# Attention and two mixture layers on one core: row numbers copied by VectorE, block 1 mixed ahead of the first bend

## What is computed

```python
# layer 0, after the attention; x: (16, 128, 128)
topk_val, topk_idx = lax.top_k(x @ gate_w + gate_b, 2)
combine = sum(one_hot(topk_idx, 24) * softmax(topk_val)[..., None], axis=-2)
h = gelu(einsum('bsd,edf->besf', x, w1) + b1)          # 24 experts, 128 -> 512
y = einsum('besf,efd->besd', h, w2) + b2               # 512 -> 128
x2 = x_in + einsum('bse,besd->bsd', combine, y) + x
# layer 1
scores = einsum('bsa,a->bs', tanh(x2 @ W1 + b1), v)
p = softmax(where(mask, scores[:, None, :], -1e30), axis=-1)
pooled = einsum('bjl,bld->bjd', p, x2) / cnt
# then 8 experts of width 176 (two for each token) and a shared network on pooled, added to x2
```

## Time and profile before

| what | us |
|---|---|
| median of 3 runs | 454.02 |
| lowest and highest run | 451.75, 457.33 |
| span of the profiled execution | 429.2 |
| busy: PE, DVE, ACT, POOL | 375.2, 278.9, 247.4, 197.5 |

### The profile page before, as it was taken

How to read it: one execution, slowest core, us unless ns; L and a number is a source line. 1 busy time by engine, 2 the same in 40 slices (tenths; PEclk the granted TensorE clock), 3 DMA queues, 4 the chain that set the end, 5 groups by cost and what they waited for, 6 DMA issues and landing times.

```text
span 429.2 us, 10202 instructions
## 1 busy us (share of the span) xinstructions
PE 375.2 (87%) x2637; PEld 270.4 (63%) x2637; DVE 278.9 (65%) x1132; ACT 247.4 (58%) x743; POOL 197.5 (46%) x273
## 2 busy tenths in 40 slices
PE   4999999899999995799998998479988779899960
PEld 4456556556666652689998997145565457677650
DVE  4566888888878888376555666369566536365562
ACT  2688788788887891546555564328874124344420
POOL 5421254444334434544554555223737506466561
PEclk9999999999999996599999999569999999899995
DMA  7603999678888404467767675320101122232354
GB/s 150 95 15 97 391 279 251 165 166 199 195 204 182 89 20 136 113 160 180 215 165 199 173 175 155 106 94 21 57 26 52 48 52 72 69 79 76 81 172 147
DMA packets 61072, 57.14 MB, mean 133 GB/s; under 512 B 6042, under 2 KB 49703, under 8 KB 60768
## 3 DMA queue, kind: packets, MB, share of 16 engines
q1 hardware_dynamic: 56288, 48.10, 45.1%
q0 software_dynamic: 4736, 8.47, 5.8%
HBM read 36.12 MB, written 21.73 MB: 135 GB/s over the span
## 4 chain that ended last, share of the span: by engine, by line
PE 58%; issue 12%; DMA 9%; DVE 8%; POOL 6%; ACT 4%; SPq 1%; POOLq 1%; DVEq 0%; ACTq 0%
PE bank L764 13%; PE bank L773 6%; PE bank L896 5%; PE bank L787 5%; PE bank L901 5%; DMA layer_outputs<-w_all 3%; POOL layer_outputs L744 3%; PE bank L1023 3%; DMA w_all<-layer_rows 2%; POOL layer_outputs L702 2%; PE bank L1103 2%; DMA qexp<-layer_outputs 2%; PE bank L804 2%; PE bank L818 2%; PE bank L871 2%
## 5 line engine op out<-in xcount | busy, mean ns | idle before, releaser
L1151 ACT ACTIVATE ps<-bank,ntop 128x128 f32<-128x128 f32 x256 | 73.4, 378 | 11.8 <-DVE ntop L1414 10.1
L1218 ACT ACTIVATE hT<-bank,w 128x128 f32<-128x128 f32 x176 | 50.8, 368 | 40.4 <-PE bank L896 40.1
L764 PE MATMUL bank<-qexp 128*128 128x512 f32 x128 | 67.8, 612 | 0.5 <-ACT ps L1151 0.5
L744 POOL DMA_INDIRECT layer_outputs<-w_all x40 | 39.9, 997 | 39.1 <-DVE w_all L1917 21.7
L773 PEld LDWEIGHTS bank<-ident,ps 128*128 128x128 f32 x256 | 31.9, 141 | 33.3 <-issue 29.8
L896 PE MATMUL bank<-xT,w 128*128 128x128 f32 x352 | 49.1, 284 | 2.8 <-DMA w<-in_L_ffn_w_dram 1.2
L1160 ACT ACTIVATE pT<-bank 128x512 f32<-128x512 f32 x64 | 38.6, 603 | 19.1 <-PE bank L773 18.1
L1413 DVE TENSOR_REDUCE mx<-bank 128x4 f32<-128x512 f32 x64 | 43.7, 683 | 8.5 <-PE bank L764 7.0
L668 POOL TENSOR_TENSOR qexp<-kA,rowmask 128x512 f32<-128x512 f32 x15 | 15.6, 1037 | 69.1 <-DVE kA L1498 69.1
L896 PEld LDWEIGHTS bank<-xT,w 128*128 128x128 f32 x352 | 44.6, 199 | 4.0 <-issue 2.6
L732 POOL DMA_INDIRECT layer_rows<-rows_all,places x32 | 30.8, 961 | 24.7 <-DVE rows_all L1791 10.3
(11 more groups left out here) (328 smaller groups left out, 814.6 us busy)
## 6 DMA issues: line engine op xcount, KB each, us to landing
w<-in_L_ffn_w_dram SPq DMA_DIRECT2D x44, 258.0 KB, 3.4
layer_rows<-fill SPq DMA_DIRECT2D x10, 910.0 KB, 9.1
w_all<-in_L_ffn_w_dram SPq DMA_DIRECT2D x24, 256.0 KB, 4.7
qexp<-layer_outputs SPq DMA_DIRECT2D x8, 512.0 KB, 4.0
xt<-layer_rows SPq DMA_DIRECT2D x45, 65.0 KB
w_all<-layer_rows SPq DMA_DIRECT2D x40, 65.0 KB, 1.9
xfT<-in_xfT_dram SPq DMA_DIRECT2D x16, 128.0 KB, 2.4
layer_rows<-fill SPq DMA_DIRECT2D x1, 1560.0 KB, 12.3
```

What stands on the lines that cost most here:

```text
L744: g.indirect_dma_start(ys1_dram, bass.IndirectOffsetOnAxis(ap=xt1[r][:, P:P + 1].bitcast(U32), axis=0), yb1[r][:, :], None, bounds_check=Y ...
L764: pe.matmul(psA[g % 2][:, :], qexp[b % 2][:, g, :], kexp[b % 2].rearrange("p g k -> p (g k)"), start=True, stop=True).then_inc(a_in_ps, 1)
L1151: m = s.activation(ps[g % 2][:, t, :], psA[g % 2][:, t * P:(t + 1) * P], ACT.Exp, bias=ntop[:, h:h + 1])
L1218: s.activation(hT[r % 2][:, c, :], banks[c][:, 0:P], ACT.Gelu, bias=w1[r][:, F0 + c:F0 + c + 1]).then_inc(gelu_done, 1)
```

## The change

It has two parts. In the extra tiles the copy of the row numbers moves from GpSimd, where it followed the send of the tile before, to VectorE, where it stands ahead of the result of the same tile; the semaphore `copied` goes. In the middle stage VectorE mixes block 1 ahead of `bend(0)` and not behind the two memsets that follow it, and `mixing` gets a wait for its own results of the block before (`x2_ready`).

```diff
             nr = pool.value_load(rounds[0:1, 0:1], min_val=EXTRA_MIN // RING, max_val=EXTRA_MAX // RING)
-            g.tensor_copy(row_r[0][:, :], idx[:, E0:E0 + 1]).then_inc(copied, 1)
             with pool.Fori(0, nr) as n:
                 for r in ring:
-                    j = RING * n + r
-                    pool.wait_ge(y_ready, E0 + 1 + j)
-                    pool.wait_ge(copied, j + 1)
+                    pool.wait_ge(y_ready, E0 + 1 + RING * n + r)
                     carry(pool)
                     send_results(row_r[r][:, 0:1], r)
-                    q = (r + 1) % RING
-                    pool.wait_ge(y_out[q], 16 * (E0 // RING + n + (r + 1) // RING))
-                    g.tensor_copy(row_r[q][:, :], idx[:, bass.ds(j + E0 + 1, 1)]).then_inc(copied, 1)
...
             def extra_y(n, r):
-                dve.wait_ge(weights_kept, 2 * (RING * n + r + 2))
+                j = RING * n + r
+                dve.wait_ge(weights_kept, 2 * (j + 2))
+                dve.wait_ge(y_out[r], 16 * (n + first_extra))
+                dve.wait_ge(xT_ready, E0 + j + 1)
+                carry(dve)
+                v.tensor_copy(row_r[r][:, :], idx[:, E0 + j:E0 + j + 1] if isinstance(j, int) else idx[:, bass.ds(E0 + j, 1)])
                 take_y(E0 + RING * n + r, r, n + first_extra, b2_r[r])
...
                 dve.wait_ge(xa_ready, k + 1)
+                if k >= 1:
+                    dve.wait_ge(x2_ready, k)
                 for t in range(BLK):
...
             mixing(0)
+            mixing(1)
             cb.join()
             bend(0)
             for t in ht1:
                 v.memset(t[:, F1:2 * P], 0.0).then_inc(ht1_zero, 1)
             dve.wait_ge(ht1_zero, 2)
-            mixing(1)
             weigh(0)
```

More of the change, by code:

```diff
@@ L317, in attention_moe_kernel @@
         lists_full = sem("lists_full")
-        copied = sem("copied")
         xt_in = [sem(f"xt_in{r}") for r in range(RING)]
```

## The result

| | before | after |
|---|---|---|
| median of 20 runs each, us | 454.50 | 459.07 |
| lowest and highest | 449.88, 457.99 | 453.57, 466.02 |
| span of the profiled execution | 429.2 | 459.5 |

The ratio is 1.0092 with a 95% interval of 1.0061 to 1.0123: 4.6 us slower by the medians, where 0.7 was forecast with a range up to 457.8. It lies within 2%, but outside the range. Runs of one kernel fall into a faster and a slower group, and every ratio in this document is that of the fast ones alone, so it isn't the quotient of the medians beside it.

What follows compares the result with a forecast made beforehand. It took the seam into the second layer to be bound by GpSimd's last send, block 1's load and mixing(1), not PE. Terms -3.65, +3.25 and +1.10 gave +0.7 us, 454.7 us from 454.0, range 451.4 to 457.8.

Steps and rivals of the forecast that it cites:

- The send 3.65 us earlier: End of the extra tiles: without its copy GpSimd starts the last send at 268.1 in place of 271.75.
- I cost the extra tiles at nothing: Extra tiles: VectorE's added copies, taken as 0.2 us each, are hidden in its spare time and add nothing.
- the last send near 268.1: Sign at the loop's end: GpSimd's last send starts there, or 1.0 to 1.6 us after the last result starts.
- the last result at 266.6: Sign at the loop's end: VectorE's last extra result still starts at this time, within 0.2 us.
- rival 4: Extra tiles: VectorE becomes the bound if its copy costs up to 1.04 us; 11 us more, 465 us, chance 0.03.
- rival 3: Extra tiles: sends held by copies of the second weights, so GpSimd still lags; +4.3 us, 458.3 us, chance 0.12.
- 3.25 + 1.10: Seam, us added at PE: bend and exponentials behind block 1's mixing, then GpSimd's addition in VectorE's way.
- `mixing(1)` at 274.4: Seam: block 1's load and mixing move along with the last send, so mixing starts 3.65 us before 278.08.
- The round of bend and exponentials behind M: Seam: bend(0) through exponentials, 3.10 us, now follows M, the end of block 1's mixing (277.55); costs 3.25 us.
- The collision: Seam: GpSimd's residual addition for block 3 holds up weigh(0)'s first VectorE operation; PE starts 1.10 us later.
- The clock: PE behind the seam: full clock may return later relative to the work, adding 0 to 0.5 us; outside the sum.
- The descriptor rule: Extra tiles: by the skill page, VectorE's SBUF copies block GpSimd's descriptor writes, some 2.5 us more per send; not adopted.

Runs made afterwards that it cites:

- e_dummy: Kernel before plus a VectorE copy of the row numbers ahead of each extra tile's result, into a spare tile nobody reads; ratio 0.9937, repeat 1.0005.
- c_before: Kernel before, unchanged, run and profiled a second time; median 451.39 us against 452.65 for the kernel before beside it, ratio 1.0003.
- c_after: Changed kernel with both parts, run and profiled a second time; median 460.69 us against 452.65 for the kernel before, ratio 1.0140.
- e_afill: Changed kernel plus two unread matmuls on PE between turn_x2(1) and turn_weights(0); median 454.90 us against 452.63 for the kernel before, ratio 1.0092.

## Why the prediction failed

- **The send 3.65 us earlier: wrong, by the term "I cost the extra tiles at nothing".** The steps on GpSimd held: a send starts 1.15 us after its result (1.06 forecast), none waits for a copy, and it follows the send before after 0.30 (0.64 assumed). VectorE's copy took 0.15 us (0.2) and is hidden, as e_dummy shows. But the last result came 2.9 us later than in c_before (271.16, 268.27), and this ate the gain; the last send starts at 272.43 in both. I had asked what the copy does to VectorE, and not what earlier sends do to the loop that makes the results, probably through SP's queue. Of the tests that the prediction named, the last send near 268.1 and the last result at 266.6 both failed, and the second says why. None of its cases had it: rival 4 had later results, but by a slow copy, and its sign (results over 1.95 us apart, here 41.1 / 19 = 2.16) came true without its cause.
- **What that one term is worth.** With -3.65 put at nothing, the prediction's own sum is 3.25 + 1.10 = 4.35 us, the size of its rival 3, and the medians differ by 4.6. At PE the weights of block 0 came 3.5 and 4.2 us later than in c_before (286.44, 287.13, 282.96). So the missing gain is about the whole error, unless the clock takes a part of it.
- **`mixing(1)` at 274.4: wrong for that reason alone**; it came 6.2 us after the last send started, as before (278.41 - 272.20; 6.33 in the earlier trace rows).
- **The round of bend and exponentials behind M: right.** M to PE's `turn_weights(0)` was forecast as 5.40 us (282.95 - 277.55) and is 4.92 (286.44 - 281.52), where c_before has about 1.1. With the gain gone, all of it beyond that 1.1 is a loss.
- **The collision: right, its victim chance.** GpSimd's addition runs beside `weigh(0)` in both executions of the changed kernel. In c_after it is the first operation that is held, 1.14 us in place of 0.15, as forecast; in the other the third, 1.34 in place of 0.69. Timelines of VectorE in c_after, and of GpSimd and VectorE in the first execution of after:

```profile
284.99 1.14 DVE L1744 TENSOR_TENSOR sc_<-psum_,count 128x4 f32<-128x4 f32 x1 [1.60 <-ACT qexp L1240]
```

```profile
284.64 1.20 POOL L698 TENSOR_TENSOR xr<-xr,rows_all 128x512 f32<-128x512 f32 x1 [4.05 <-DMA xr<-in_x_dram]
...
285.04 1.34 DVE L1746 TENSOR_TENSOR w_all<-qexp,rs_ 128x512 f32<-128x512 f32 x1
```

- **The clock: more than was allowed for, its price open.** It was left out of the sum as 0 to 0.5 us; the estimate above makes it 2. I had taken the idle time between `turn_x2(1)` and `turn_weights(0)` as 5 us with no consequence beyond itself. Rows show the full clock at 299 to 301 instead of 285, and further stretches at half clock behind it (17 us between 310 and 362, where c_before has 10). That the clock is a part of the 4.6 us isn't shown: in e_afill it is back at 287, and the ratio is still 1.0092.
- **The descriptor rule: not seen.** The 20 sends took 967 ns at the least and 1147 at the most, although eight of them overlap one of VectorE's 128x512 copies. The Trainium skill (SBUF — State Buffer, "A bandwidth-pool intuition that's wrong (but worth ruling out)") gives 3100 ns for a DMA that takes 620 alone, and has it wait until VectorE's instruction is done. It gives no length for that instruction, and a wait that ends with a copy of 0.43 us can't cost the 2.5 us that the prediction took from it; what the trace has is 0.18. Rival 3, which named 458.3 us, came nearest the time, by luck: GpSimd doesn't lag, the results do.
- **Base and range.** The sum was made on an execution 21 us shorter than a usual one. In its middle stage, from block 0's weights to the plan, it took 57.6 us against the 71.8 of c_before, and in its loop none of SP's pauses followed a send. Both effects that the account above turns on, SP's pauses and stretches at half clock in the middle stage (none between 310 and 362), were absent from the only trace at hand. The 24.8 us between its span and the median were the warning: in every other run the time is 1.8 us above the span. A range made from the bounds of that one trace could not hold what it didn't contain, and its upper end, 457.8, even left out the prediction's own third case (458.3, chance 0.12).

What stays open: why the first execution was 21 us shorter; how a longer lag of the sends shortens the extra tiles; and whether the clock costs time here, since the matmuls that bring it back leave no loss in one kernel and a ratio of 1.0092 in the other.

## What to carry to other kernels

A queue that lags behind may be harmless slack: before its lag is removed, ask what its transfers will then meet, and which engine bounds the loop that feeds it (here SP's queue of loads). A gap in TensorE's work where it is at half clock can keep it there: two unread matmuls in the gap brought the clock back here, and whether that saves time has to be measured in the kernel at hand. And when the span of the one profile lies far from the median of the runs, the trace is not of the execution that is timed, and no sum on it is safe to a few microseconds.

## What the runs showed of the hardware

SP's sequencer stood still for about 0.5 us behind 11 of 16 indirect sends of GpSimd in c_before and 13 of 15 in c_after (pauses up to 0.72 us when two sends start 1.3 us apart), on register instructions too, and behind none of 15 in the rare first execution. Two such sends in a row can start 1.27 us apart. Two 128x512 matmuls in PE's idle time went with a return of the full clock at 287 instead of 301 us. An operation of VectorE as small as 128x4 took 1.14 us in place of 0.15 where it met a 1.2 us addition of GpSimd. The Trainium skill (GPSIMD Engine Reference, "1. Specifications") says that the two contend when VectorE reads two SBUF inputs, and by that row the trace agrees.
